# A one-core MetaFormer layer: edge counts beside the first front end, copies of idle keys on ScalarE, a part of the edge scatter in the rank stage

## The reference

```python
corr = jnp.einsum('bmf,bnf->bmn', x3, x3) / F
s = -jnp.sort(-corr, axis=-1)
ranks = jnp.round(jnp.linspace(1.0, M - 1, NB_POOLS)).astype(jnp.int32)
pooled = jnp.take(s, ranks, axis=-1)
```

```python
e = jax.nn.leaky_relu(a_src[src] + a_dst[dst], negative_slope=0.2)
e_max = jax.ops.segment_max(e, dst, num_segments=M)
ee = jnp.exp(e - e_max[dst])
denom = jax.ops.segment_sum(ee, dst, num_segments=M)
alpha = ee / (denom[dst] + 1e-16)
msg = h[src] * alpha[:, :, None]
agg = jax.ops.segment_sum(msg, dst, num_segments=M).reshape(M, HEADS * NUM_EXPERTS) + b_gat
```

## Time and profile before

| what | us |
|---|---|
| median of 3 runs (lowest, highest) | 30719.29 (30713.63, 30737.62) |
| the profiled execution, its span | 30707.68, 30706.0 |
| VectorE busy in the span | 27866.9 (91%) |
| TensorE matmul | 26132.4 (85%) |
| ScalarE | 20334.5 (66%) |
| POOL | 19826.0 (65%) |

### The profile page before, as it was taken

The page is one execution under the profiler, slowest core; times in us unless marked ns, Lnnn a source line. Parts: engine busy times, 40 slices in busy tenths (PEclk is TensorE's granted clock), DMA queues, the critical chain, the costliest instruction groups (busy, mean ns, idle before and its releaser), DMA issues. The chain is left out here.

```text
span 30706.0 us, 514061 instructions
## 1 busy us (share of the span) xinstructions
PE 26132.4 (85%) x182003; PEld 12435.8 (40%) x182004; DVE 27866.9 (91%) x31378; ACT 20334.5 (66%) x30319; POOL 19826.0 (65%) x9076
## 2 busy tenths in 40 slices
PE   3888889989999999999999999989999999982473
PEld 2555543333333333333333333333333333332473
DVE  6888858999999999999999999999999999996435
ACT  1777777767767767767776776767777777763720
POOL 0000007898888888888888888888888898402610
PEclk8999999999999999999999999999999999996655
DMA  2000000000000000000000000000000000000104
GB/s 93 2 2 2 2 19 4 7 7 7 7 7 7 12 7 7 7 7 7 7 12 7 7 7 7 7 6 7 13 7 7 7 6 7 7 5 13 15 11 136
DMA packets 651242, 393.57 MB, mean 13 GB/s; under 512 B 425132, under 2 KB 604336, under 8 KB 646448
## 3 DMA queue, kind: packets, MB, share of 16 engines
q1 hardware_dynamic: 338034, 311.42, 3.2%
q0 software_dynamic: 290304, 22.40, 1.1%
q10 hardware_dynamic: 20288, 25.70, 0.2%
HBM read 196.49 MB, written 162.34 MB: 12 GB/s over the span
## 5 line engine op out<-in xcount | busy, mean ns | idle before, releaser
L1584 POOL DMA_INDIRECT sorted_d<-word_s,place_s x8192 | 18974.3, 2316 | 2642.8 <-issue 2476.8
L1496 ACT ACTIVATE z<-psum 128x1024 f32<-128x1024 f32 x10089 | 10181.7, 1054 | 2004.0 <-PE psum L1223 1258.5
L1395 DVE TENSOR_TENSOR arena<-arena 128x1024 f32<-128x1024 f32 (+16 forms) x5760 | 10843.3, 1883 | 442.8 <-ACT arena L1492 397.0
L1396 DVE TENSOR_TENSOR arena<-arena 128x1024 f32<-128x1024 f32 (+16 forms) x5760 | 10837.1, 1881 | 0.0
L1223 PE MATMUL psum<-z,net 64*64 64x512 f32 x72504 | 9163.8, 601 | 140.3 <-ACT z L1496 111.2
L1496 ACT ACTIVATE cst<-psum 128x1024 f32<-128x1024 f32 x5015 | 5303.4, 1058 | 979.2 <-PE psum L1223 635.0
L1223 PE MATMUL psum<-cst,net 64*64 64x512 f32 x36040 | 4826.4, 602 | 77.9 <-ACT cst L1496 51.0
L1223 PEld LDWEIGHTS psum<-z,net 64*64 64x64 f32 x72504 | 2425.6, 131 | 5275.3 <-issue 5178.5
L1216 PE MATMUL psum<-rows,arena 128*128 128x256 f32 x8192 | 2017.6, 402 | 1629.4 <-ACT arena L1492 1597.1
L1578 POOL DMA_DIRECT2D word_s<-words_d x64 | 37.5, 586 | 4830.5 <-ACT cst L1496 4702.1
L1038 ACT ACTIVATE arena<-cst,arena 128x128 bf16<-128x128 f32 x8320 | 2632.8, 389 | 610.1 <-PE psum L966 513.4
(11 more groups left out here) (231 smaller groups left out, 23519.1 us busy)
## 6 DMA issues: line engine op xcount, KB each, us to landing
sorted_d<-word_s,place_s POOLq DMA_INDIRECT x8192
y_d<-ys SPq DMA_DIRECT2D x256, 256.0 KB
arena<-y_d SPq DMA_DIRECT2D x64, 1024.0 KB, 5.5
arena<-in_x SPq DMA_DIRECT2D x34, 512.0 KB, 5.1
x<-in_x SPq DMA_DIRECT2D x65, 256.0 KB
xnt_d<-arena SPq DMA_DIRECT2D x32, 512.0 KB, 3.1
hk_d<-arena SPq DMA_DIRECT2D x32, 512.0 KB, 4.3
arena<-hk_d SPq DMA_DIRECT2D x4, 4096.0 KB
```

What stands on the lines that cost most here:

```text
L1395: nc.vector.tensor_tensor(hi_out, hi_in, lo_in, ALU.max)
L1396: return nc.vector.tensor_tensor(lo_out, hi_in, lo_in, ALU.min)
L1496: last = nc.scalar.activation(flat, bank, ACT.Abs)
L1584: pool.indirect_dma_start(out=b.sorted_d[:, :], out_offset=bass.IndirectOffsetOnAxis(ap=place_s[:, s, j:j + 1], axis=0), in_=word_s[:, s, ...
```

## The change

Five edits, all in the blocks named above.

1. `prepare`: the token phase comes first and is pipelined by one group (statistics and deviation of the next group ahead of newton of this one; the x load of a slot is issued once it is normalised). The edge counts come after it, TensorE's product in bank 6. Between their subs TensorE issues the 256 ticks of pair 0's front end (`FIRST_PAIR`): none in the first ten subs, then spread evenly over the other 118. ScalarE makes the copies, SP the stores of words and the loads of edges.

```diff
             with sp.Fori(0, N_X) as i:
                 for s in range(2):
-
-                    sp.wait_ge(turned_copied, i * 2 + s + 1)
-                    tok = (i * 2 + s) * 512
+                    k = i * 2 + s
+                    sp.wait_ge(normed, k + 1)
+                    nxt = ((k + 2) % (TILES // 4))
+                    sp.dma_start(xs[s], x_q[bass.ds(nxt, 1)].rearrange("o p q d -> (o p) q d")).then_inc(x_in[s], 16)
+
+                    sp.wait_ge(turned_copied, k + 1)
+                    tok = k * 512
                     sp.dma_start(b.xnt_d[:, :, bass.ds(tok, 512)], xt[s]).then_inc(xt_out[s], 16)
                     sp.dma_start(b.hk_d[:, :, bass.ds(tok, 512)], ht[s]).then_inc(xt_out[s], 16)
-
-                    nxt = ((i * 2 + s + 2) % (TILES // 4))
-                    sp.dma_start(xs[s], x_q[bass.ds(nxt, 1)].rearrange("o p q d -> (o p) q d")).then_inc(x_in[s], 16)
+            for s in range(2):
+                sp.wait_ge(xt_out[s], 32 * N_X)
+            sp.dma_start(b.xnt[:], b.hk_d[:, :, 0:M]).then_inc(b.hk_in, 16)
+            sp.dma_start(b.rows[:], b.xnt_d[:, :, 0:2 * P]).then_inc(b.rows_in, 16)
...
+            def statistics(t, s, round_):
+
+                dve.wait_ge(x_in[s], round_ * 16)
+                for q in range(4):
+                    last = nc.vector.bn_stats(stat[:, q, :], xs[s][:, q, :])
+                t.then(last)
+                dve.sem_inc(b.settled[0], 1)
+                for q in range(4):
+                    last = nc.vector.bn_aggr(mv[:, s, q, :], stat[:, q, :])
+                t.then(last)
+                nc.vector.tensor_scalar(var[:, s, :], mv[:, s, :, 1], LN_C_EPS, None, ALU.add).then_inc(stats_ready, 1)
+
+            statistics(Tally(dve, dve_step, base=x_base), 0, 1)
+            with dve.Fori(0, N_X) as i:
+                for s in range(2):
+                    k = i * 2 + s
+                    t = Tally(dve, dve_step, base=k * X_STEPS + (x_base + 2))
+                    statistics(t, 1 - s, i + (1 + s))
+                    dve.wait_ge(std_ready, k + 1)
+                    newton(nc, t, rstd, rtmp, var[:, s, :], std[:, s, :])
+
+                    dve.wait_ge(turned, i * 2)
+                    for q in range(4):
+                        last = nc.vector.tensor_scalar(xn[s][:, q, :], xs[s][:, q, :], mv[:, s, q, 0:1],
+                                                       rstd[:, q:q + 1], ALU.subtract, ALU.mult)
+                    last.then_inc(normed, 1)
...
+                    for g in range(8):
+                        last = nc.tensor.matmul(psum[:, 6, 0:64], l16[:, g * 128:g * 128 + 128],
+                                                l8[:, g * 64:g * 64 + 64], start=(u == 0 and g == 0),
+                                                stop=(u == SUBS - 1 and g == 7))
+                    last.then_inc(hot_used, 1)
+                    upto = max(k * SUBS + u + 1 - ALONE, 0) * len(FIRST_PAIR) // (2 * N_E * SUBS - ALONE)
+                    for s, n in FIRST_PAIR[done:upto]:
+                        front_matmuls(nc, b, pe, z, 0, s, n)
+                    done = upto
 
```

```diff
-                dve.wait_ge(place_made, n + 1)
+                    dve.wait_ge(rank_used, (k + 1) * GROUPS)
+                    v = places[:, s, :]
+                    nc.vector.tensor_scalar(over[:, s, :], v, BIG, 2.0 * BIG, ALU.is_lt, ALU.mult).then_inc(over_made, 1)
+                    dve.wait_ge(over_made, k + 1)
+                    dve.wait_ge(place_out[s], i * 16)
+                    nc.vector.scalar_tensor_tensor(place_i[:, s, :], v, -BIG, over[:, s, :], ALU.add,
+                                                   ALU.add).then_inc(place_made, 1)
+
...
+
+        @block.gpsimd
+        def _(pool):
+            with pool.Fori(0, EARLY_SUPERS // 2) as i:
+                for s in range(2):
+                    pool.wait_ge(place_out[s], (i + 1) * 16)
+                    scatter(nc, b, pool, i, s)
+            for k in range(SCAT_SEMS):
+                pool.wait_ge(b.scattered[k], EARLY_SUPERS * SCAT // SCAT_SEMS * 16)
+
```

```diff
+    work = [(1 if s >= FIRST_MERGE else (M - LO) / M) if s < N_FULL else 0.5 for s in range(N_STAGES)]
+    CARRY_AT = {(p, which): round(H_BODY / BODY_PAIRS * sum(work[:first_of(p) + which + 1]) / sum(work))
+                for p in MERGES for which in range(2)}
...
+            def carry(i, p, which):
+
+                s = first_of(p)
+                act.wait_ge(sorted_, (i * N_FULL + (s + 1)) * 2)
+                to = 2 * (M - LO) if s < FIRST_MERGE else 2 * M
+                nc.scalar.activation(edges_of(keys[(s + 1) % 2][:, 0:to], p, which),
+                                     edges_of(keys[s % 2][:, 0:to], p, which), ACT.Copy).then_inc(carried, 1)
+
+            def carries(i, place):
+                for (p, which), at in CARRY_AT.items():
+                    if place == at:
+                        carry(i, p, which)
```

```diff
+            def spread_share(i, s):
+
+                dve.wait_ge(got_in[s], (i + 1) * (16 * EQ))
+                dve.wait_ge(other_ready, i * N + (s + 1))
+                dve.sem_inc(b.settled[0], 1)
+                for h in range(HEADS):
+                    for q in DVE_Q:
+                        last = nc.vector.tensor_scalar(spread[s][:, h, q, :], other[s][:, q, :], MASKED,
+                                                       got[s][:, q, h:h + 1], ALU.mult, ALU.add)
+                last.then_inc(share_ready[s], 1)
+
             with dve.Fori(0, rounds) as i:
+                for s in (0, 1):
+                    spread_share(i, s)
                 for s in R:
```

```diff
+                    last = nc.vector.tensor_reduce(
+                        looked[:, s * EQ:(s + 1) * EQ, :],
+                        psum[:, 4 + s, 0:E_AT].rearrange("p (q j f) -> p q f j", q=EQ, j=3), AX.X, ALU.add)
+                dve.wait_ge(got_in, (i + 1) * 16)
+                t.then(last)
+                t.then(nc.vector.tensor_tensor(z, got[:, :, 0:HEADS], looked[:, :, 0:HEADS], ALU.add))
+                leaky(dve, t, z)
+                t.mark(nc.vector.tensor_tensor(z, z, looked[:, :, HEADS:], ALU.subtract))
+                dve.wait_ge(exp_ready, i + 1)
+                t = Tally(dve, part_step, base=i * 4)
+                t.then(nc.vector.tensor_tensor(
+                    value[:, :, HEADS:].rearrange("p n (h e) -> p n h e", h=HEADS),
+                    got[:, :, HEADS:HEADS + GAT].rearrange("p n (h e) -> p n h e", h=HEADS),
+                    value[:, :, 0:HEADS].unsqueeze(3).broadcast_to([P, NE, HEADS, EXPERTS]), ALU.mult))
+                t.then(nc.vector.tensor_copy(parts[:, :, 0, :], value))
+                t.then(nc.vector.tensor_tensor(rest, value, parts[:, :, 0, :], ALU.subtract))
+                t.then(nc.vector.tensor_copy(parts[:, :, 1, :], rest))
+                nc.vector.tensor_tensor(parts[:, :, 2, :], rest, parts[:, :, 1, :], ALU.subtract).then_inc(
+                    value_ready, 1)
```

555 lines of the change are left out of this document (289 added, 266 removed).

## The result

The change takes 36756.99 us (median of four runs, 35902.69 to 38302.16), the kernel before 30719.19. The ratio of 1.177 [1.163, 1.192] counts only the two faster of the four runs (35903 and 36422 us). The forecast was 30470, so the sign is wrong and the size by 6 ms. Four runs of one kernel that spread over 2400 us are a finding by themselves: the kernel before spreads over 24. The profile is of the 38302 us run; I read from it where time goes, not how much on the average.

The account below looks back on a forecast made before the run. VectorE, 99% busy through 64 back-to-back sorts, was taken as the bound. Terms -15 + 147 + 56 - 285 + 294 - 45 - 400 = -248 gave 30460 us, 30470 on the median's scale; range 29650 to 30950 (forecast's own 30250 to 30700).

Parts of the forecast that it names:

- what one costs VectorE no row of this stage shows: Rank stage: VectorE's cost of 1792 indirect DMAs, taken as 0.04 us each, +70, bounds 0 and +180.
- it fits up to 1.90 us each: Rank stage end: POOL's 1792 DMAs finish in time up to this pace; 1.74 taken, done 290 us early.
- rival (b): Scatter outlasts the rank stage: at 2.16 us per DMA the block ends 470 us late, 30900 us; chance 0.13.
- (c): Rank stage: POOL holds VectorE for each indirect DMA's length, at least 0.966 us, 1731 in all: 32130 us; chance 0.04.
- VectorE now waits 6.7 us: Each sort, ahead of stage 2: VectorE waits for ScalarE's carry (128,0), which stands behind the corr copy of place 3.
- Prepare +119 (+132): Prepare block: token phase -15 by pipelining, edge counts with pair 0's front end +147.
- Start of the sort stage: Sort 0 ends at T+470 instead of T+760, held by its first carry until T+125: -285 us.
- segment_max +8 (-45): segment_max: a quarter of ScalarE's spreads moved to VectorE saves 1 us in each of 47 rounds, -45.
- Per sort +8.8 (+4.8): Sort stage: copies off VectorE -8.0, waits +6.7 and +5.4; with the front end's loop 368.5 us, +4.8 each.
- The others are 13 to 17 us early: Sort stage: ScalarE's copies other than (128,0) and (256,0) are ready before their stage ends, costing VectorE 0.
- The sum for the front end's loop: Sort stage: 336.4 us plus 13.5 of copies and three waits of some 5 us comes to 366 to 371.
- segment_sum -165 (-400): segment_sum: bf16 products and a round of 11.2 us instead of 20.0, 47 rounds, -400 (-330 to -450).

Follow-up runs that it names:

- a1_after: The change rerun unaltered on a chip where the kernel before takes 30456 us: 30596 us, ratio 1.0047.
- e9_places: Change without early supers, POOL starting after pair 1's wires, p = 128 copies on VectorE, others at later places, segment_sum indices read ahead: 29436 us, 0.966.
- c2_early14: c1_best with the change's 14 early scatter supers back in the rank stage at full pace: 31915 us, 1.039 of the kernel before.
- c1_best: "Put together": change without early supers, POOL gated, p = 128 copies on VectorE, others moved, segment_max spreads on ScalarE, segment_sum indices read ahead: 29592 us, 0.9637.
- e3_carry_dve: The change with the ten copies of idle keys per sort back on VectorE: 33651 us, 1.095 of the kernel before.
- e4_gate: The change with no scatter in the rank stage and POOL starting only when pair 1's wires are copied: 35786 us.
- e2_cap2: The change with at most two scatter DMAs in flight in both stages: 31921 us, 1.039 of the kernel before.

## Why the prediction was wrong

By block, in us. "Slow" and "fast" are the service of an indirect DMA in the rank stage, 1.70 us and at most 1.31.

| block | before | change, slow | change, fast | put together, slow |
|---|---|---|---|---|
| prepare | 706 | 835 | 825 | 829 |
| rank | 3591 | 5807 | 3510 | 3451 |
| sort stage | 23724 | 29001 | 23987 | 23043 |
| segment_max | 1277 (fast 1019) | 1430 | 1027 | 1276 |
| segment_sum | 955 | 786 | 787 | 529 |

**The step that failed** is "what one costs VectorE no row of this stage shows", with its bounds of 0 and +180, and beside it "it fits up to 1.90 us each". I bounded an indirect DMA by how much longer it makes VectorE's ops, and asked whether POOL gets through in time. Both came out as forecast: POOL got through with its 1792 at 4055 us in the slow place, and where service is fast they cost the rank stage 3510 - 3455 = 55 us (a1_after against e9_places, one chip) for 70 forecast. L1065 lasts 0.689 us, late increments or not, and L1029 0.300 at most for 0.280. What decides is a third thing, to which the prediction gave no term: while POOL issues its DMAs faster than they are served, what waits for TensorE is held up, in the rank stage until some 50 us behind the end of the product. It costs 2340 us in the rank stage (c2_early14 against c1_best) and, in the run profiled, 29001 - 23987 = 5014 us in the sort stage (against a1_after). My rival (b), the scatter outlasting the stage, priced waiting for landing alone; (c) had 0.97 us of VectorE per DMA by the port, and the loss of 2340/1792 = 1.3 us each is near that number but not that mechanism: VectorE's ops are not longer by more than 0.02, it is TensorE's increments that are late, to ScalarE as well as to VectorE, and in the fast place nothing of the kind is lost. So the rule of the Trainium skill that I weighed ("SBUF — State Buffer", "Who interferes with whom") is not what these runs show.

**What ties it to the sorts.** "VectorE now waits 6.7 us" was right in itself. I cost that wait as time of VectorE only. It is also time in which POOL runs free. e3_carry_dve (no such wait, no disturbed sort after the second), e4_gate (waits, disturbed without any cold start), e2_cap2 (the same waits with at most two DMAs in flight, none disturbed) and c1_best (places moved, 2.3 us of waits per sort left, none disturbed but the first) show together that it takes both the waits and the free POOL. That one sets off the other within a sort is my reading of them.

**Sizes, from the undisturbed run in the fast place** (forecast in brackets). Prepare +119 (+132): right. Start of the sort stage 464 us to the end of sort 0 (470): right. segment_max +8 (-45), and +153 in the slow place, where POOL's gathers are bound by service. There VectorE's share of the spreads is what costs, for without it c1_best has 1276; why it costs so much was not shown. Per sort +8.8 (+4.8). VectorE's waits in 28 sorts of the change show why:

```profile
...
DVE arena L1511 <- ACT arena L1612: 293.8, 56, 11.7
DVE rs L1675 <- ACT std L1579: 213.2, 28, 7.6
...
```

213.2/28 = 7.6 for newton, forecast 7.3 (5.4 + 1.9). 293.8/28 = 10.5 for ScalarE's copies, forecast 6.7: 7.9 of it stands ahead of stage 2, and 2.5 ahead of stage (1024,256), for which I had put 0. "The others are 13 to 17 us early" was counted on a ScalarE without copies and waits; with them it has lost its lead. The sum for the front end's loop had a slip besides: 336.4 + 13.5 + 15 is 365, not 366 to 371; and 322 us over 32 iterations of the token phase are 10.06 each, not 9.85. Neither changes the outcome.

segment_sum -165 (-400). A round takes 16.1 us, not 11.2. Its groups, 37150 to 37850 us:

```profile
...
L2046 PE MATMUL psum<-arena 128*128 x696 | 48.7, 186 | 111.9 <-issue 80.0 <-ACT arena L2070 32.0
...
L2016 DVE TENSOR_TENSOR arena<-arena,psum 128x60 f32 x174 | 37.8, 217 | 179.9 <-DVE arena L2016 121.7 <-PE psum L2053 58.2
...
```

The four adds are 0.22 us each, but each waits 0.94 us, and TensorE's look-ups 0.7, where the program reads the tile index from memory into a register. I had "four adds 0.8" and nothing for the reads; reading them ahead, the only edit to this block, brings 787 down to 529 us.

Rank without scatter is 3451, not 3577: with the one-hots moved, VectorE waits less for TensorE ahead of the reductions. I had not seen that term; that moving them is the reason was not tested by itself. The sum in the fast place, 119 - 75 + 263 + 8 - 165 = +150, meets the measured +140. The +263 of the sort block is about 62 x 8.8 for the sorts less some 275 for the earlier end of sort 0. So even without the late increments the forecast of -248 fails, on two terms above all: the sorts (+8.8 each, forecast +4.8) and segment_sum (-165, forecast -400).

## What to carry to other kernels

Ask of every engine that issues small DMAs in a row whether something holds its pace below the rate at which they are served. If what holds it is another engine's work, then waiting that an edit gives to that engine can set the DMAs free, and a cost that looked like 6 us per sort turned into hundreds here. The rate of service is found in the profile as issues per microsecond over a long stretch plus the wait for landing behind it, never in the issuing engine's own busy time.
